# A transformer block with a 16-expert layer: biases in a last weight row, zero pads written once, tables waited for one by one, and GpSimd combining gathered rows

## The reference, cut to what matters

```python
x = x + 0.5 * moe(layernorm(x))     # x: (16, 256, 128) float32, 4096 tokens of 128
x = x + attention(layernorm(x))     # 16 heads of 8, causal, with biases
x = x + 0.5 * moe(layernorm(x))     # the same expert weights again

def moe(xt):                        # 16 experts, the best 2 for each token
    logits = xt @ Wg.T + bg
    top_vals, top_idx = top_k(logits, 2);  rw = softmax(top_vals)
    gu = xt @ Wgu[e] + bgu[e];      gate, up = gu[..., ::2], gu[..., 1::2]
    gate = min(gate, 7);            up = clip(up, -7, 7)
    out_e = ((up + 1) * gate * sigmoid(1.702 * gate)) @ Wd[e] + bd[e]
    return sum over the two experts of rw * out_e
```

## Time and profile before

| | |
|---|---|
| median of three runs | 763.55 us (762.5 to 764.29) |
| the profiled execution | 764.87 us, its span 763.0 us |
| PE, PEld | busy 526.7 and 352.4 us |
| DVE, ACT, POOL | busy 524.5, 316.6 and 297.4 us |

### The profile page before, as it was taken

The page is one execution under the profiler, slowest core; times in us unless marked ns, Lnnn a source line. Parts: engine busy times, 40 slices in busy tenths (PEclk is TensorE's granted clock), DMA queues, the critical chain, the costliest instruction groups (busy, mean ns, idle before and its releaser), DMA issues.

```text
span 763.0 us, 19935 instructions
## 1 busy us (share of the span) xinstructions
PE 526.7 (69%) x6287; PEld 352.4 (46%) x6287; DVE 524.5 (69%) x2691; ACT 316.6 (41%) x602; POOL 297.4 (39%) x308
## 2 busy tenths in 40 slices
PE   3357629999747979788888977888832049999200
PEld 2234218887523546454544544555421038888100
DVE  6865418888777787678767776789746038888722
ACT  1001018888514545445444544334401048888000
POOL 2777750021441424141414102017777200057774
PEclk9999999999969898999899989788965569999755
DMA  9533134455465261435234333301112325566522
GB/s 270 149 97 94 52 96 117 139 161 155 150 208 181 69 194 57 135 119 165 87 112 141 124 100 113 111 2 53 50 48 83 97 65 144 147 171 183 149 80 62
DMA packets 112611, 90.27 MB, mean 118 GB/s; under 512 B 12357, under 2 KB 104970, under 8 KB 112266
## 3 DMA queue, kind: packets, MB, share of 16 engines
q1 hardware_dynamic: 78218, 59.77, 26.0%
q0 software_dynamic: 8192, 16.79, 7.9%
q10 hardware_dynamic: 26112, 12.59, 5.6%
HBM read 44.98 MB, written 44.11 MB: 117 GB/s over the span
## 4 chain that ended last, share of the span: by engine, by line
PE 43%; DVE 21%; issue 13%; POOL 11%; SPq 4%; ACT 3%; DMA 3%; DVEq 1%; ACTq 0%; POOLq 0%
PE banks L1537 10%; POOL by_token L505 8%; DVE by_token L789 5%; PE banks L1548 4%; PE banks L1525 3%; POOL rows_by_expert L543 3%; PE banks L1453 3%; SPq L408 3%; PE banks L1311 2%; PE banks L1501 2%; PE banks L1287 2%; PE banks L1261 2%; DVE x_resident L739 2%; DVE by_token L916 2%; PE banks L1445 2%
## 5 line engine op out<-in xcount | busy, mean ns | idle before, releaser
L789 DVE CUSTOM_DVE_ANT_0 by_token<-banks,konst_sb 128x128 f32<-128x128 f32 (+1 forms) x512 | 147.0, 352 | 29.2 <-issue 28.8
L543 POOL DMA_INDIRECT rows_by_expert<-by_token,posi x120 | 116.2, 968 | 57.2 <-issue 35.0
L1537 PE MATMUL banks<-xT,pT 128*64 128x128 f32 x1536 | 109.3, 286 | 33.6 <-ACT pT L710 17.7
L710 ACT ACTIVATE pT<-w_experts 128x384 f32 x192 | 90.0, 515 | 77.5 <-DMA tab<-tabc 61.9
L610 ACT ACTIVATE pT<-banks 128x1536 f32<-128x1536 f32 x64 | 92.8, 1449 | 54.2 <-PE banks L1289 54.2
L1537 PEld LDWEIGHTS banks<-xT,pT 128*64 128x64 f32 x1536 | 85.5, 141 | 50.6 <-ACT pT L710 33.9
L505 POOL DMA_INDIRECT by_token<-results_by_tile,tilepos x64 | 61.2, 957 | 95.7 <-DMA results_by_tile<-ysb 76.7
L505 POOL DMA_INDIRECT yg<-results_by_tile,tilepos x64 | 61.9, 967 | 75.6 <-DMA results_by_tile<-ysb 57.2
L1124 DVE SCALAR_TENSOR_TENSOR sig<-banks,sig 128x256 f32<-128x256 f32 x96 | 40.4, 421 | 48.6 <-ACT sig L720 47.7
L1548 PE MATMUL banks<-pT,gT 128*64 128x128 f32 x768 | 59.4, 276 | 4.5 <-DVE ysb L1141 4.5
L604 ACT ACTIVATE mT<-banks 128x256 bf16<-128x256 f32 x64 | 24.5, 383 | 90.5 <-PE banks L1236 90.3
(11 more groups left out here) (160 smaller groups left out, 1077.5 us busy)
## 6 DMA issues: line engine op xcount, KB each, us to landing
xt<-rows_by_expert SPq DMA_DIRECT2D x192, 64.0 KB
results_by_tile<-ysb ACTq DMA_DIRECT2D x96, 128.0 KB
q_stack<-q_by_part SPq DMA_DIRECT2D x8, 1024.0 KB, 7.5
k_stack<-k_by_part SPq DMA_DIRECT2D x8, 1024.0 KB, 6.3
q_by_part<-q_parts SPq DMA_DIRECT2D x16, 384.0 KB, 3.4
k_by_part<-k_parts SPq DMA_DIRECT2D x16, 384.0 KB, 2.8
rows_by_expert<-zeros SPq DMA_DIRECT2D x65, 64.0 KB
x_resident<-in_x SPq DMA_DIRECT2D x8, 256.0 KB, 5.4
```

The source lines that it names most:

```text
L543: pool.indirect_dma_start(out=rows_dram, out_offset=bass.IndirectOffsetOnAxis(ap=posi[:, c:c + 1], axis=0), in_=rows_of(f, q)[:, i, :], in ...
L710: last = nc.scalar.activation(w_tile[:, 2 * k + i, :], w_all[:, bass.ds(held[key][k % 2 * 2 + i], EW)], ACT.Identity)
L789: last = nc.vector.tensor_tensor_reduce(masked[:, (3 * g + qt) * P:(3 * g + 2 * qt + 1) * P], of, lag, 1.0, NEG * NEG_BELOW, ALU.add, ALU. ...
L1537: last = nc.tensor.matmul(bank[2 + k % 2][h * HALF:(h + 1) * HALF, at:at + P], w_tile[:, 2 * k + i, which * F + h * HALF:which * F + (h + ...
```

## The change

1. **Last-row biases.** Since a normalised row adds up to zero, its last element can be dropped if the last row of the weights is subtracted from the 127 others. The last element of each row is set to 1.0 and the last row of the weights holds the bias. The last rows of `Wg`, `Wgu` and `W_attn` are loaded a second time, broadcast to 127 partitions (16 KB to each for `Wgu`). DVE subtracts them: `adjust(0..3)` of 1024 columns each behind `top2` of quads 3 to 6, `adjust_attention` (384 columns) in quad 2, one small one in `setup`. `column_sums`, the bias product in `values`, the bias operands of L593, L777 and L716, and the addition of `bg` go. `normalise` writes 127 columns. `split_biases` is left for `b_proj` only and moves in front of `read_ranks`.
2. **Pads zeroed once.** An expert's tiles are aligned to the end of its rows, so that its first tile reaches back into the 128 rows ahead of its region. One DMA of 2 MB at the start zeroes these 32 places for good; `zero_tiles` and the DMA of the region ends go. `counts` gets a second small product, `table` a small addition.
3. **Tables one by one.** ACT and DVE wait before each pass for that pass's own table.
4. **GpSimd combines the first layer.** POOL runs `combine` behind its gathers: one product of 1024 columns and two additions of 512. The second layer's combining stays on DVE.

```diff
@@ sync: loads at the start
-            sp.dma_start(bg[:, :], b_g.partition_broadcast(P)).then_inc(s_const, 16)
+            sp.dma_start(wg[LAST:C, :], b_g).then_inc(s_const, 16)
+            sp.dma_start(wg_last[:, :], w_g[LAST:C, :].rearrange("a e -> (a e)").partition_broadcast(LAST)).then_inc(s_const, 16)
...
+            sp.dma_start(gu_last[:, :], w_gu[LAST:C, :].rearrange("a w -> (a w)").partition_broadcast(LAST)).then_inc(s_wexp, 16)
+            sp.dma_start(w_of_expert[LAST:C, :, 0:2 * F], b_gu.rearrange("(o e) w -> o e w", o=1)).then_inc(s_wexp, 16)
...
+            sp.dma_start(w_in_last[:, :], w_attn[LAST:C, :].rearrange("a w -> (a w)").partition_broadcast(LAST)).then_inc(s_watt, 16)
...
+            sp.wait_ge(s_pool, 1)
+            sp.dma_start(rows_dram[0:SIDES * E * REGION, :].rearrange("(r w) c -> w r c", w=REGION)[0:P, :, :],
+                         zeros[:, :].unsqueeze(1).to_broadcast([P, SIDES * E, C])).then_inc(s_zero, 16)
@@ table_of
-                sp.wait_ge(s_ends, p + 1)
-                sp.dma_start(tab[0:1, g, 2 * TILES:TABW], zrow[:, :]).then_inc(s_tab_ends, 16)
-                sp.wait_ge(s_tab_ends, 16 * (p + 1))
...
-                zero_tiles(sp, g)
@@ gpsimd
+            def combine(x):
+                pool.wait_ge(a_got, (x + 1) * (16 * QUAD * TOPK))
+                of_token = a_yg.rearrange("p (n k) c -> p n k c", k=TOPK)
+                mine = xr[:, x * QUAD:(x + 1) * QUAD, :]
+                nc.gpsimd.tensor_tensor(of_token, of_token, wts[:, :, x * QUAD:(x + 1) * QUAD].rearrange("p k n -> p n k").unsqueeze(3).to_broadcast([P, QUAD, TOPK, C]),
+                                        ALU.mult).then_inc(a_half, 1)
+                pool.wait_ge(a_half, 2 * x + 1)
+                nc.gpsimd.tensor_tensor(mine, mine, of_token[:, :, 0, :], ALU.add).then_inc(a_half, 1)
+                pool.wait_ge(a_half, 2 * x + 2)
+                nc.gpsimd.tensor_tensor(mine, mine, of_token[:, :, 1, :], ALU.add).then_inc(a_comb, 1)
...
                     gather_pair(0)
+                    combine(0)
                     root_of_pair(0)
                     gather_pair(1)
+                    combine(1)
...
                         if x + 2 < B // 2:
                             gather_pair(x + 2)
+                            combine(x + 2)
@@ copy_weights (ACT); evac_y (DVE) alike
-                    if p % SIDES == 0 and isinstance(t, int) and (t, k) == (0, 0):
-                        act.wait_ge(s_tab, 32 * (p + 2))
+                    if isinstance(t, int) and (t, k) == (0, 0):
+                        act.wait_ge(s_tab, 32 * (p + 1))
@@ vector
                 if steps.combine is not None:
-                    combine(steps.combine)
                     stats(steps.combine)
...
-                    last = nc.vector.tensor_scalar(xa[:, i, :], row(x, i), a_mv[:, i, 0:1], a_rs[:, i:i + 1], ALU.subtract, ALU.mult)
+                    last = nc.vector.tensor_scalar(xa[:, i, 0:LAST], row(x, i)[:, 0:LAST], a_mv[:, i, 0:1], a_rs[:, i:i + 1], ALU.subtract, ALU.mult)
...
                 def adjust(n):
-                    dve.wait_ge(s_fix, n + 1)
-                    nc.vector.tensor_tensor(w_of[:, 2 * n:2 * n + 2, 0:2 * F], bank[6 + n % 2].rearrange("p (n w) -> p n w", n=2),
-                                            w_of[:, 2 * n:2 * n + 2, 0:2 * F], ALU.add).then_inc(s_fixed, 1)
+                    dve.wait_ge(s_wexp, 80)
+                    nc.vector.tensor_tensor(w_of, w_of, gu_last[:, n * 8 * F:(n + 1) * 8 * F].rearrange("p (e w) -> p e w", e=4),
+                                            ALU.subtract).then_inc(s_fixed, 1)
+
+                def adjust_attention():
+                    dve.wait_ge(s_watt, 64)
+                    nc.vector.tensor_tensor(w_in[0:LAST, :], w_in[0:LAST, :], w_in_last[:, :], ALU.subtract).then_inc(s_asetup, 1)
...
                         top2(q)
+                        if q == 1:
+                            split_biases()
+                        if q == 2:
+                            adjust_attention()
+                        if 3 <= q < 7:
+                            adjust(q - 3)
                         read_ranks(q)
                         positions(q)
...
-                        if q >= NQ - E // 4:
-                            adjust(2 * (q - NQ + E // 4))
-                            adjust(2 * (q - NQ + E // 4) + 1)
@@ tensor
             def values(x, at=7):
-                nc.tensor.matmul(bank[at].rearrange("p (n c) -> p n c", c=C), ones[0:3, :],
-                                 bias3[0:3, E * BW:E * BW + C].unsqueeze(1).to_broadcast([3, QUAD, C]), start=True, stop=False)
...
-                    if f == 0 and q > NQ - E // 4:
-                        column_sums(2 * (q - 1 - NQ + E // 4))
-                        column_sums(2 * (q - 1 - NQ + E // 4) + 1)
```

More of the change, by code:

```diff
@@ L38 @@
 TILES = TSIDE * TOPK + E
-TABW = 2 * TILES + E
+TABW = 2 * TILES
+LAST = C - 1
 UNROLL = 8
@@ L46 @@
 EW = 2 * F + C
-BW = 2 * F
 WB = EW + C
@@ L247, in build_block @@
         spare = sb("spare", [P, 1])
+        gu_last = by_token[0:LAST, 0:E * 2 * F]
+        wg_last = rest[0][0:LAST, 0:E]
+        w_in_last = rest[0][0:LAST, E:E + 3 * C]
         a_yg = sb("yg", [P, QUAD * TOPK, C])
@@ L403, in stack_rest @@
                     stack_pair(sp, t, half)
[L405 to L408, removed]
         @block.sync
@@ L430, in _ @@
[L430 to L433, removed]
+            sp.dma_start(w_out[:, :], w_proj).then_inc(s_watt, 16)
+            sp.wait_ge(s_pool, 1)
+            sp.dma_start(rows_dram[0:SIDES * E * REGION, :].rearrange("(r w) c -> w r c", w=REGION)[0:P, :, :],
+                         zeros[:, :].unsqueeze(1).to_broadcast([P, SIDES * E, C])).then_inc(s_zero, 16)
@@ L473, in _ @@
                 table_of(first)
-                sp.wait_ge(s_zero, 16 * (1 + E * (first + 1)))
+                if f == 0:
+                    sp.wait_ge(s_zero, 16)
                 sp.wait_ge(s_scat[0], 16 * TOPK * TSIDE * (f + 1))
@@ L592, in high @@
                 beyond_first(act, a_spread[which], x * 48)
-                nc.scalar.activation(parts[which][:, 0, :], bank[at][:, :], ACT.Identity, bias=bqk[:, which:which + 1]).then_inc(a_high[which], 1)
+                nc.scalar.activation(parts[which][:, 0, :], bank[at][:, :], ACT.Identity).then_inc(a_high[which], 1)
             def evac_v(x, half, at=7):
@@ L732, in row @@
                 return xr[:, bass.ds(x * QUAD + i, 1), :].rearrange("p a c -> p (a c)")
[L734 to L745, removed]
             def settle():
@@ L776, in split_rest @@
                 beyond_first(dve, a_low[which], x)
[L777 to L778 removed]
+                nc.vector.tensor_tensor(rest[which][:, :], bank[at][:, :], parts[which][:, 0, :], ALU.subtract).then_inc(a_rest[which], 1)
             def row_max(t, s):
@@ L1186, in values @@
                         last = nc.tensor.matmul(bank[at][h * HALF:(h + 1) * HALF, i * C:(i + 1) * C], xaT[:, i * P + h * HALF:i * P + (h + 1) * HALF],
-                                                w_in[:, 2 * C:3 * C], start=False, stop=i == QUAD - 1)
+                                                w_in[:, 2 * C:3 * C], start=i == 0, stop=i == QUAD - 1)
                 last.then_inc(a_v, 1)
@@ L1481, in counts @@
                 def counts(p):
-                    nc.tensor.matmul(bank[6][0:E, 0:P], macc[:, before(QSIDE * (p % SIDES + 1) - 1) + 1, :], ones[:, :], start=True, stop=True).then_inc(s_count, 1)
+                    nc.tensor.matmul(bank[6][0:E, 0:P], macc[:, before(QSIDE * (p % SIDES + 1) - 1) + 1, :], ones[:, :], start=True, stop=True)
+                    nc.tensor.matmul(bank[6][:, P:P + E], ones[:, :], macc[:, before(QSIDE * (p % SIDES + 1) - 1) + 1, :], start=True, stop=True).then_inc(s_count, 1)
                     pe.wait_ge(s_ntile, p + 1)
@@ L1490, in _ @@
                     units()
-                def column_sums(n):
-                    if n == 0:
-                        pe.wait_ge(s_wexp, 48)
-                        pe.wait_ge(s_bias3, 48 + 48)
-                    if n >= 2:
-                        pe.wait_ge(s_fixed, n - 1)
-                    for i in range(2):
-                        o, e = bank[6 + n % 2][:, i * 2 * F:(i + 1) * 2 * F], 2 * n + i
-                        nc.tensor.matmul(o, share[0:3, :], bias3[0:3, e * BW:e * BW + 2 * F], start=True, stop=False)
-                        last = nc.tensor.matmul(o, spread[:, :], w_all[:, e * WB:e * WB + 2 * F], start=False, stop=True)
-                    last.then_inc(s_fix, 1)
                 for q in range(f * MERGED, NQ + 1):
```

106 lines of the change are left out of this document (45 added, 61 removed).

## The result

The changed kernel is slower: 835.07 us, median of four runs (834.1 to 838.89), against 763.92 (762.5 to 764.66) for the kernel before in the same comparison. The ratio is 1.0943, 95% interval [1.0903, 1.0983]. The forecast was 670. The profiled execution has a span of 837.0 us, 74.0 above the 763.0 of before; at 838.89 us it is the longest of the four, 3.8 above their median.

The account below looks back on a forecast made before the run. No engine was taken to bound the whole: nearly empty stretches before expert products, routing, and PE-DVE handoffs in attention. Terms 36.5 + 27.8 + 15.6 + 4 + 3.8 + 7, less 1 for loads, gave 93.7 off, so 670 us; range 657 to 690.

Parts of the forecast that it names:

- Loads: Start of kernel: 2.4 MB more loads land at 37, `adjust_attention` in quad 2 waits about 1 us more.
- the loads come late: Rival: `gu_last` broadcast at 73 GB/s takes 28 us, DVE stands in quad 2, 24 us late; 694 us, chance 0.09.
- wrong it would be if DVE idles in quad 2 for a DMA: Sign against the forecast: DVE idle in quad 2 of the first routing stage, waiting for a load; no size given.
- The slower side: Outcome slower than the kernel before, expected if POOL's `combine` took 26 us or more; chance 0.02.
- First layer: First routing stage to first expert product: shorter quads, earlier tables and no wait behind zero writes; 36.5 us off.
- Second layer: Second layer's table ready to first expert product: store no longer behind zero writes, product at 592.2 instead of 620.00; 27.8 us.
- Combine: First-layer attention: moving `combine` to POOL takes 2.6 us off PE's wait for L810, six times; 15.6 us.
- pass 1: Two combines in expert pass 1 leave DVE, 4.6 us of its time, taken at 4 us.
- values: The 3-row bias product in `values`, 0.602 us seven times, goes; 3.8 us off.
- clock: Attention: with shorter waits PE runs at 2.4 GHz in the v products, 1.2 us per half-turn; 7 us, bounds 0 and 12.
- POOL starves: Rival: POOL gets SBUF only while DVE idles, `combine` takes 19 us, total 718; at 30 us, 785; slower has chance 0.02.

Follow-up runs that it names:

- the mended kernel: Changed kernel with broadcasts to 128 partitions and weight loads cut 112 + 15, so no DMA over 127; 667.15 us against 764.04 before on the third chip.
- the two combine runs: First-layer combining back on DVE in the mended kernel: 884.85 us, 19.5 above it; combining moved to POOL in the kernel before: 919.94 us, ratio 0.9802.

## Why the prediction was wrong, point by point

The sum of 93.7 had one term that was wrong by far, the loads. It was charged 1 us and measured 170.0.

- **Loads: wrong, and by its size it turned the sign.** The step read "the core loaded 250 GB/s; 2.4 MB more land at 37". The 250 came from loads over 128 partitions and was applied to loads over 127, as if bytes alone set the time. At 127 the rate is 24. I counted the load that is added and not the one that changed its shape: `w_gu`'s own 2 MB, the same bytes as before less one row, cost as much as the addition. The rival "the loads come late" named the place (DVE in quad 2) and had 24 us, from a rate of 73 GB/s, at 0.09; and "wrong it would be if DVE idles in quad 2 for a DMA" is what the profile shows. The slower side was given to POOL, which was not slow. In the mended kernel the term is 3.7, and the whole is 667 where 670 was forecast. That the bytes land at 37 was right once no load went over 127 partitions: in the mended kernel `adjust_attention` starts at 37.48.
- **First layer: right.** From 111.45 to 243.41 - 170.0 = 73.4 are 38.0; predicted 36.5.
- **Second layer: right.** From POOL's last `rstd` of the second routing, which is in both chains (565.95 before, 666.79 after), to the first product (620.00 and 692.96): 54.05 and 26.17, so 27.9 off; predicted 27.8. From there to the end: 143.0 before, 144.0 after, 1.0 lost.
- **Combine, pass 1, values, clock: right in sign and about right in size.** From the first product of layer 1 to that `rstd`: 454.5 before, 423.4 after, 31.1 off; predicted 15.6 + 4 + 3.8 + 7 = 30.4. That it is so close is in part luck: in the profiled executions of the changed and the mended kernel on the third chip the stretch takes 418.2 and 417.7, which is 36.3 and 36.8 under the same 454.5, so it is known to some 6 us only, and what brings the 6 is not shown. The chain jumps at the turns of the attention loop, at "issue" rows that are 78.42 apart before and 68.13 after:

```profile
306.96 3.28 issue
...
385.38 3.36 issue
...
565.95 1.68 POOL rstd L535
```

```profile
429.18 3.00 issue
...
497.31 3.10 issue
...
666.79 1.68 POOL rstd L528
```

  That is 10.3 a turn and 5.15 a half-turn, where the forecast's 15.6 + 3.8 + 7 over six or seven half-turns are 4.3. (The last lines are the `rstd` of the point before.) PE's waits for `add_attention` shrank from 21.5 in six to 5.7 in six, 0.95 each where 1.0 was forecast; that is 15.8 off, where 15.6 were forecast. The v products are back at 2.4 GHz: the granted clock is 1.00 in the window shown, in which the 16 of a half-turn run, and half of them last 273 ns, where the median of the earlier trace rows was 421. The 16 took 1.87 to 1.98 us in six half-turns and take 1.09 in six, 5.2 of the 7 forecast for the clock. (Waits; window; line L1170.)

```profile
PE banks L1220 <- DVE x_resident L797: 5.7, 6, 1.1
```

```profile
412.00:414.00 2.00, 2.00 (x35) 1.33 (x33) 1.93 (x13) 1.51 (x2) 1.69 (x2) 1.00 0.99 322
```

```profile
L1170 PE MATMUL banks<-w_attn_sb,xnT x112: 272/273/476, 380.3 to 593.6; 128*64 128x128 f32 x112
```

- **POOL starves: didn't happen.** Its product and two additions of a pair (groups by line and form: busy, mean ns):

```profile
L502 POOL TENSOR_TENSOR yg<-yg,wts 128x1024 f32<-128x1024 f32 x8 | 15.3, 1908 | 14.6 <-DMA yg<-results_by_tile,tilepos 14.6
L507 POOL TENSOR_TENSOR x_resident<-x_resident,yg 128x512 f32<-128x512 f32 x8 | 10.7, 1333 | 0.6
L505 POOL TENSOR_TENSOR x_resident<-x_resident,yg 128x512 f32<-128x512 f32 x8 | 10.4, 1297 | 0.6
```

  4.54 us a pair beside a busy DVE; predicted 4.7. `adjust` took 1218 ns four times; predicted 1.2 to 1.4 us.

The stretches add up: 170.0 - 38.0 - 31.1 - 27.9 + 1.0 = 74.0, the difference of the spans. How the 31.1 divides among its four parts is shown in part: the shorter waits and v products are measured in the traces, but what each takes off the end is not, and the two combine runs bear on it on the slower chips only.

## What to carry to other kernels

Look at the partition count of every DMA that an edit reshapes, not only at its bytes: 128, 126 and 112 kept the DMA engines full, 127 kept one busy, at less than a tenth of the rate (24 GB/s against 287 to 333). Where "all rows but the last" is wanted, load 112 + 15 (or broadcast to all 128 and use 127). When a change goes wrong by a large amount, find the longest single wait and subtract it: if the rest then agrees with the working, one term is wrong, and the repair is small.

## What the runs showed of the hardware that was not expected

- A 2.08 MB DMA over 127 partitions ran at 24 GB/s (DMA share 0.07) and held back SP itself: the issue behind it took 87.69 us, and in the kernel before with this one load cut the issues of its two parts took 95.56. With only the weights mended the issue behind `gu_last` took 45.02 us and that of `w_d`, behind `w_in_last`, 35.52, though `w_d` goes over 128 partitions. So everything later in SP's list waited, short and fast loads too.
- The same mended kernel took 865.64 us on the second chip and 667.15 on the third. Its instructions last as long (DVE's group of 512 row maxima: 147.1 and 147.0 us busy), but on the second chip the group idles 74.9 us for nothing that the profile shows, against 13.0 on the third, and 11% of the chain that ended last is put down to "another core or an unknown queue", which has no share in the chain on the third. Idle rows of 8.8 us stand twice in each turn of attention (45.05 and 40.95 us apart), where the changed kernel in the first comparison has one of 3.0 to 3.1 a turn; so not only the jump of the loop costs more.

```profile
L779 DVE CUSTOM_DVE_ANT_0 by_token<-banks,konst_sb 128x128 f32<-128x128 f32 (+1 forms) x512 | 147.1, 353 | 75.1 <-issue 74.9
```

```profile
311.03 8.83 issue
...
356.08 8.79 issue
...
397.03 8.73 issue
```

  Whether this is the chip or something around it was not tried and stays open. It is the reason for reading the runs of the first two chips by their ratios.
